# Second layer of a two-layer kernel: the result made from rows of x1 and scattered straight to the output, in place of a turned-back tile added to x1

## The reference, cut to what matters

```python
def _L1_cond_ref(x, c, weight, c_weight, bias):
    out = lax.conv_general_dilated(x, weight, window_strides=(1,), padding=[(4, 4)], ..., feature_group_count=4)
    ctx = jnp.einsum('nd,od->no', c, c_weight)
    return out + ctx[:, :, None] + bias[None, :, None]

def _L1_ffn_ref(x, up, down, perm):           # up [16, 128, 512], down [16, 512, 128]
    unperm = jnp.argsort(perm)
    t = x.reshape(b * l, Dm)[:, perm].reshape(b * l, h, d)
    t = jax.nn.gelu(jnp.einsum('bhd,hdm->bhm', t, up), approximate=False)
    t = jnp.einsum('bhm,hmd->bhd', t, down).reshape(b * l, h * d)
    return t[:, unperm].reshape(b, l, Dm)

x = x + _L1_ffn_ref(_L1_cond_ref(x, cond_128, ...), L1_ffn_up, L1_ffn_down, L1_ffn_perm)
```

## Time and profile before

| | |
|---|---|
| median of 3 runs | 2507.34 (2507.33 to 2508.14) |
| the profiled execution, its own time | 2513.49 |
| its span in the profile | 2511.7 |
| mean granted TensorE clock | 0.989 of full |
| busy: TensorE matmul, VectorE, ScalarE, GpSimd | 97%, 68%, 44%, 37% |
| HBM read and written | 309.72 MB and 228.61 MB |

### The profile page before, as it was taken

The page is one execution under the profiler, slowest core; times in us unless marked ns, Lnnn a source line. Parts: engine busy times, 40 slices in busy tenths (PEclk is TensorE's granted clock), DMA queues, the critical chain, the costliest instruction groups (busy, mean ns, idle before and its releaser), DMA issues.

```text
span 2511.7 us, 37065 instructions
## 1 busy us (share of the span) xinstructions
PE 2432.4 (97%) x11130; PEld 2010.9 (80%) x11130; DVE 1713.9 (68%) x2449; ACT 1113.7 (44%) x1850; POOL 938.1 (37%) x826
## 2 busy tenths in 40 slices
PE   8899999999999999999999988999999999999985
PEld 6788888888888888887888866888888888888864
DVE  6665555875555855558544665778888888888865
ACT  3221211321212322223222356777777777777753
POOL 2275654556645255323233311222222222222331
PEclk9999999999999999999999999999999999999988
DMA  8965554755543767657555665468888888888898
GB/s 301 326 214 187 199 174 159 258 177 205 202 163 132 269 219 225 204 178 258 178 172 172 194 196 153 141 189 244 242 245 248 240 240 243 245 246 245 231 245 255
DMA packets 397563, 540.90 MB, mean 215 GB/s; under 512 B 37016, under 2 KB 262640, under 8 KB 397360
## 3 DMA queue, kind: packets, MB, share of 16 engines
q1 hardware_dynamic: 295872, 309.50, 43.0%
q10 hardware_dynamic: 77376, 152.17, 16.2%
q0 software_dynamic: 24112, 76.80, 9.9%
HBM read 309.72 MB, written 228.61 MB: 214 GB/s over the span
## 4 chain that ended last, share of the span: by engine, by line
PE 88%; DMA 5%; DVE 3%; issue 2%; SPq 1%; ACT 1%; POOL 0%; ACTq 0%; DVEq 0%; POOLq 0%
PE ps_c L463 45%; PE ps_up L1401 13%; PE ps_y L1411 13%; PE ps_c L1426 9%; PE ps_v L441 4%; PE ps_c L429 3%; DMA u_s<-z_d,idx 1%; DVE w_lo L1006 1%; PE ps_up L1426 1%; SPq L88 1%; DMA rear<-x_d 1%; DVE ring_lo L953 1%; DMA w_hi<-y_d 1%; DMA x_n<-in_up 0%; DVE x_s L1002 0%
## 5 line engine op out<-in xcount | busy, mean ns | idle before, releaser
L463 PE MATMUL ps_c<-w_hi,ring_hi 128*128 128x512 f32 x1792 | 703.9, 393 | 4.9 <-DVE r_early L1002 3.6
L463 PE MATMUL ps_c<-w_hi,ring_lo 128*128 128x512 f32 x1792 | 698.0, 390 | 0.0
L463 PE MATMUL ps_c<-w_lo,ring_hi 128*128 128x512 f32 x1792 | 697.9, 389 | 0.0
L613 ACT ACTIVATE ring_hi<-raw_n 128x512 fp32r<-128x512 f32 x382 | 239.6, 631 | 852.2 <-DVE raw_n L944 232.1
L1581 DVE TENSOR_TENSOR g_lo<-kern,g_hi 128x512 fp32r<-128x512 f32 x512 | 349.2, 687 | 80.3 <-ACT g_hi L1483 71.3
L463 PEld LDWEIGHTS ps_c<-w_hi,ring_hi 128*128 128x128 f32 x1792 | 336.8, 188 | 75.8 <-DVE ring_lo L953 4.7
L463 PEld LDWEIGHTS ps_c<-w_hi,ring_lo 128*128 128x128 f32 x1792 | 336.5, 188 | 69.8
L463 PEld LDWEIGHTS ps_c<-w_lo,ring_hi 128*128 128x128 f32 x1792 | 336.8, 188 | 67.5
L1383 POOL DMA_INDIRECT y_d<-y_room,idx x128 | 131.8, 1030 | 651.7 <-ACT y_room L1516 584.9
L1002 DVE TENSOR_TENSOR r_early<-ps_c,r_early 128x512 f32<-128x512 f32 x256 | 176.4, 689 | 275.9 <-PE ps_c L463 275.9
L1479 ACT ACTIVATE kern<-ps_up 128x512 f32<-128x512 f32 x512 | 304.5, 596 | 118.4 <-PE ps_up L1401 102.8
(11 more groups left out here) (188 smaller groups left out, 3628.0 us busy)
## 6 DMA issues: line engine op xcount, KB each, us to landing
u_d<-raw_n ACTq DMA_DIRECT2D x64, 512.0 KB, 3.2
x_d<-r_early ACTq DMA_DIRECT2D x128, 256.0 KB, 3.5
raw_n<-u_d SPq DMA_DIRECT2D x64, 512.0 KB, 3.6
x_d<-x_s ACTq DMA_DIRECT2D x126, 256.0 KB, 2.8
u_s<-x_d SPq DMA_DIRECT2D x496, 64.0 KB, 2.4
z_d<-x_s SPq DMA_DIRECT2D x120, 256.0 KB, 4.7
rear<-y_d SPq DMA_DIRECT2D x224, 128.0 KB, 3.7
rear<-x_d SPq DMA_DIRECT2D x56, 512.0 KB, 4.4
```

The lines of the kernel that those rows point to most:

```text
L463: mm = nc.tensor.matmul(bank, a[:, dc, :], w[k][:, dc, :], start=(first and dc == 0 and n == 0), stop=(dc == 3 and n == 2), skip_group_che ...
L613: nc.scalar.activation(ring_hi[g % RING][:].rearrange("p a n -> p (a n)"), factor(q, k, p), ACT.Copy).then_inc(hi_ready, 1)
```

## The change

The result of step s is now finished by rows. x1 is turned like z: `turn_x` (VectorE, 128x512) writes each unit's x1 into a tile, and SyncE stores it to `xt_d`, four more DMAs of 256 KB per tile, issued behind the four of z. `gather_row` (GpSimd) gathers the head's 128 rows of x1 by the permutation, `add_rows` (VectorE) adds the PSUM bank of down_part, and `scatter` (GpSimd) writes the sum to the output, now laid out as [8 x 2048, 512]; its index is the permutation plus 2048 times the block. The host's last reshape puts it in order. Out go: the copy of the bank by ScalarE, `y_d` and its reads, `turn_y`, the load of x1 for the pairs, `add_x1`, `store_out`, and all of the last block's own way out (its loads, the 64 transposes, 16 additions, 64 stores).

Beside this: x tiles 0 to 3 alternate between two buffers, all later ones use one; `turn_x(u)` stands first in VectorE's step from step 0 on (after turn_z in the lead) and, where a tile begins, waits until all four DMAs of the tile before have landed; SyncE's load for a unit waits for `turn_x` of the unit whose buffer it takes, too; the loads of the fourth buffer and its padding wait for the last matmul of the first layer; conv has two banks throughout; ScalarE rounds chunks 0, 2, 3 and VectorE chunk 1; the hardware loop is written out.

```diff
+    def turned_rows(self, dram, r, part):
+        return dram.rearrange("(w i r) n -> r i w n", w=WIDE, r=S)[r, :, :, part * C:(part + 1) * C]
...
+        z_tiles = [by_batch(sh.x1_s[:].rearrange("p a n -> p (a n)")), by_batch(rows[:].rearrange("p w n -> p (w n)"))]
+        x_tiles = [by_batch(x_turned[:]), by_batch(late_turned[:])]
+        ps_c = [bank(f"ps_z{j}") for j in range(2)]
...
+        def tile_of(tiles, tile):
+            return tiles[tile % 2 if tile < G else 0]
+        def last_tile_user(tile):
+            return tile - 2 if tile <= G else tile - 1
+        def tile_free(eng, stored, tile):
+            last = last_tile_user(tile)
+            if last >= 0:
+                eng.wait_ge(stored[last % 2], 64 * (last // 2 + 1))
...
         @block.sync
...
+            def load_rows(u):
+                _, b, g = place(u)
+                last = last_xp_user(u)
+                wait(sp, xlo_ready, last + 1)
+                wait(sp, xt_ready, last + 1)
+                if u == 3:
+                    sp.wait_ge(sh.item_mm, LAST)
...
+            def step(u, s):
+                if u + 4 < H + 2:
+                    load_rows(u + 4)
+                elif H <= u and u + 2 < STEPS:
+                    load_rows(u + 2)
+                if u < STEPS and u % SB == SB - 1:
+                    tile = u // SB
...
+                    sp.wait_ge(zt_ready, u + 1)
+                    store_tile(z_d, z_tiles, z_out, tile, range(2 if tile == G - 1 else S))
...
+                    sp.wait_ge(xt_ready, u + 1)
+                    store_tile(xt_d, x_tiles, xt_out, tile, range(S))
...
         @block.gpsimd
...
+            def gather_row(s):
+                h = s % H
+                block_stored(pool, xt_out, s)
+                if s >= 4:
+                    pool.wait_ge(y_out[s % 2], 16 * (s // 2 - 1))
+                nc.gpsimd.indirect_dma_start(out=rows[:, s % 4, :], in_=xt_d[s // H % 2], ...).then_inc(row_in[s % 2], 16)
+            def scatter(s):
+                h = s % H
+                pool.wait_ge(o_ready, s + 1)
+                nc.gpsimd.indirect_dma_start(out=out, ..., in_=rows[:, s % 4, :], ...).then_inc(y_out[s % 2], 16)
+            def step(u, s):
...
+                if 0 <= s + AHEAD < STEPS:
+                    gather_t(s + AHEAD)
+                if 0 <= s + 2 < STEPS:
+                    gather_row(s + 2)
+                if s >= 0:
+                    scatter(s)
...
-                    nc.scalar.activation(y_s[j], ps_y[j][:, 0, :], ACT.Copy).then_inc(y_ready, 1)
...
         @block.vector
...
+            def turn_x(u):
+                tile = u // SB
+                if u % SB == 0:
+                    tile_free(dve, xt_out, tile)
+                nc.vector.transpose(tile_of(x_tiles, tile)[:, :, u % SB, :],
+                                    xp[xp_of(u)][:, 1:Q + 1].rearrange("p (w c) -> p w c", w=WIDE)).then_inc(xt_ready, 1)
+            def add_rows(s):
+                dve.wait_ge(down_done, MC * (s + 1))
+                dve.wait_ge(row_in[s % 2], 16 * (s // 2 + 1))
+                nc.vector.tensor_tensor(rows[:, s % 4, :], ps_y[s % 2][:, 0, :], rows[:, s % 4, :], ALU.add).then_inc(o_ready, 1)
+            def step(u, s):
...
+                else:
+                    if u < STEPS:
+                        turn_x(u)
+                    if s + 2 < STEPS:
+                        split_t(s + 2)
+                    if u < STEPS:
+                        turn_z(u)
+                    if u + 1 < STEPS:
+                        split_x(u + 1)
+                for mc in range(MC):
+                    if 0 <= s + 1 < STEPS:
+                        split_g(s + 1, mc)
+                    if s >= 0 and mc == MC - 2:
+                        add_rows(s)
```

## The result

The changed kernel takes 2739.76 us (median of 4 runs, 2736.45 to 2742.75) against 2507.34 for the kernel before: 1.0928 times, 95% interval 1.0909 to 1.0947. That is 232 us longer; 163 had been forecast (2670), and 2740 lies 10 above the upper end of the range.

What follows compares the result with a forecast made beforehand. TensorE was taken to bound full steps, busy 599 of 600 us. Terms +189 +20 -19 -27 = +163 on the profiled 2513.5 gave 2676.5, and 2670 since that execution is 6.2 above the median; range 2530 to 2730.

Steps and rivals of the forecast that it cites:

- One buffer for x tiles: Full steps, tiles 5 to 31: turn_x waits for the last tile's stores, TensorE stops 4.6 us; with clock loss +189.
- The x stores go behind them: SyncE's queue at a tile's end: x's four stores follow z's and land 5.0 us later, bounds 3.74 and 6.0.
- so I add nothing: GpSimd's scatter and next gather come late once per tile, but with slack while TensorE itself stands; priced at nothing.
- the rival of the upper ends: Whole kernel: stop 5.6, clock 2.4, lead +35, ending only -5, as gathers and scatters share the engines; 2726, chance 0.10.
- The clock after a stop, 2.4: Step behind each stop: TensorE runs at a granted clock of 0.55 for 6 us, losing 2.4 us (0 to 2.4).
- The rule on 512 B: Tile stores: by the skill they'd run like larger ones, 2.8 us per tile; the trace's 176 GB/s, 6.0, was preferred.
- hidden wait: Rival, full steps: x stores land before VectorE needs them, TensorE doesn't notice; -32 us, 2475, chance 0.10.
- The lead, +20: Before full steps: x stores of tiles 0 to 3 add 14 to 24, waiting loads 0 to 10; +20 (10 to 35).
- The ending, -19: Last steps, 126.5 us long: stops mostly go as x1 loads, pair reads and output stores leave; -19 (0 to -20).
- the way out, -27: After the last matmul: 33.0 us become 5.9, add_rows plus the last scatter; -27 (-24 to -28).
- The edits priced at nothing: Full steps: VectorE, ScalarE and GpSimd changes fit under TensorE's 7.56 us, written-out loop counted at nothing; no cost.

Runs made afterwards that it cites:

- run with another source: Changed kernel, but from tile 5 on the x stores take their bytes from a weight buffer nothing rewrites, so turn_x has no wait; 2515.3 us.
- the last run: Kernel with turn_x a unit ahead throughout and the lead's x stores on GpSimd, but tile 4's back on SyncE; 2482.4 us, 0.9895 of the kernel before.
- the half store's: Changed kernel, but from tile 8 on only two of the four quarters of the x tile are stored; 2649.8 us.
- the version a step ahead: Changed kernel with turn_x one unit ahead behind split_x from step 0 on, x stores alone in their own step; 2501.0 us, 0.9975 of the kernel before.

## Why the prediction was right and wrong, point by point

- **One buffer for x tiles: right in mechanism, place and count.** Of four convolutions one is late and the step behind it slow, 27 times; VectorE stands at turn_x; eight stores go in a row. All of this was named. The run with another source shows the wait as the cause: 224 of the 232 us went with it.
- **"The x stores go behind them ... I take 5.0": this is the step that failed, by its size.** From the first z issue to turn_x it was 12.2 in the forecast and 14.6 on average over 25 tiles (15.2 in the one shown: 1872.94 to 1888.14). The z stores landed 7.8 after their first issue (forecast 7.2) and the x stores 6.8 behind them (forecast 5.0, upper bound 6.0). That bound priced x's bytes alone, at the rate of 512 B pieces, with no GpSimd transfers beside them; "so I add nothing" was said of GpSimd's lateness, and its share of the engines was named for the rival of the upper ends alone and stands nowhere in my sum. The runs show what was missing in part: the row gathers are 1.1 of the stop. The size of the pieces is 0.4 and a second queue moves only the start, while half of x's stores are 3.3. What the other gathers and scatters in the window (0.8 of 3.6 MB) cost wasn't tried, so the rest of the 2.4 is open. The stop was 6.9 and not 4.6, which is 62 us over 27 tiles. Against the forecast by the profiled executions (+163, measured +226.5) that is nearly all of the 63.5 missing; the lead's 6 more and the clock's 5 less about cancel.
- **The clock after a stop, 2.4: right.** 2.2 measured, and 2.0 of them come back when TensorE is kept at work in the stop.
- **The rule on 512 B** of the Trainium skill ("DMA: Bandwidth & Descriptors", Specifications: 512 B is the least transfer for line rate) was set aside on the strength of one window at 176 GB/s. The run with large pieces gives the rule more credit than that: larger pieces shorten the stop by only 0.4. But what it would have led to, a hidden wait, didn't come: the stores landed late with pieces of either size.
- **The lead, +20: 26 came, 29 from the end of the first layer, with parts near those forecast.** I had 14 to 24 for the stores and 0 to 10 for the loads' waits. The run without x stores has 17.8 for the stores and 11.6 for the rest; GpSimd issuing them in SyncE's place took 9.9 off. Of the rest some 5 lie where the loads wait for turn_x. The fourth buffer's wait for the first layer's last matmul was not tried by itself.
- **The ending, -19, and the way out, -27: right**, -18.4 and -26.5. The ending's gain is where it was said to be: 12.6 us of stops became 1.3, and the clock of the ending went from 0.95 to 1.00. That it is the missing loads and stores that did it is argued, since no run takes them out by themselves; the DMA engines' share fell from 0.90 to 0.49.
- **The edits priced at nothing** (add_rows, the roundings, the third indirect DMA, the written-out loop): the steps of 7.56 between the stops, and 599.5 busy us of 600 in the last run, bear out that they are hidden in full steps. In the window of the stores the third indirect DMA did have a price, the 1.1 above.
- **The rivals.** "Upper ends together" (2726) was nearest. The hidden wait needed a landing 3.5 us earlier than even the half store's; it is what the version a step ahead made true, by another order.

## What to carry to other kernels

A single buffer that is written, stored and written again is a loop; its length is the landing of the store with everything else that moves in that window, and all of it must fit between the last write and the next first one. Look at what all queues move there, the indirect ones too, and then look for another phase before looking for another buffer: here the same stores, one step earlier and alone, cost nothing in full steps. A wait at the head of an engine's list also holds up what doesn't need it, and a load that waits for a second reader of its buffer makes a loop of its own where nothing covers it. And when two profiles are compared at one instant, make sure that it is the same step in both, and that what ran ahead of it took the same time.

## What was not expected of the hardware

- Stores of 256 KB in pieces of 512 B and in pieces of 8 KB took nearly the same time beside GpSimd's transfers (14.3 and 13.8 us for the window of eight), the second with 2860 packets in place of 4758.
- Splitting the eight stores over two queues left the time from first issue to last landing at 14.2 (14.5 on one).
- Half a MB less in that window gave 3.3 us when it was stores (two of them) and 1.1 when it was gathers.
- 24 matmuls that nobody needs, run in the stop, made the kernel 50 us faster: the stops stayed (7.0 and not 6.8), and the granted clock rose (0.99 in place of 0.89 over the same window).
